# A Flamingo layer on one core: heads kept and scaled in PSUM with two banks, two score banks instead of three, an expert's low part in four pieces, and new order tables

## The reference, cut to what matters

```python
x = x + tanh(g_xattn) * attention(layernorm(x), ctx, ctx, Wq, bq, Wk, bk, Wv, bv, Wo, bo)   # 16 heads of 32
xt = layernorm(x).reshape(4096, 512)
probs = softmax(xt @ router_w + router_b)            # 8 experts
gate, idx = max(probs), argmax(probs)
y = gate * (xt @ expert_w[idx] + expert_b[idx])
x = x + tanh(g_ffn) * y
```

## Time and profile before

| | us |
|---|---|
| median of three executions | 1152.27 |
| the profiled execution | 1165.53 |
| its span, first to last instruction | 1163.8 |

### The profile page before, as it was taken

The page is one execution under the profiler, slowest core; times in us unless marked ns, Lnnn a source line. Parts: engine busy times, 40 slices in busy tenths (PEclk is TensorE's granted clock), DMA queues, the critical chain, the costliest instruction groups (busy, mean ns, idle before and its releaser), DMA issues. The chain is left out here.

```text
span 1163.8 us, 19046 instructions
## 1 busy us (share of the span) xinstructions
PE 1032.3 (89%) x5464; PEld 659.0 (57%) x5464; DVE 805.2 (69%) x1748; ACT 513.1 (44%) x920; POOL 670.6 (58%) x446
## 2 busy tenths in 40 slices
PE   3798899999998999899999998999899765789885
PEld 2554456546754674476457655765565323667674
DVE  5656655876687769767975886588667758686454
ACT  4245624564356345535544454445443435333331
POOL 3046645774587448745874685468545556554453
PEclk9898989999999999999999998999999967999988
DMA  7334222533253334233432432243223712543431
GB/s 231 76 74 121 66 67 68 141 75 98 69 138 78 91 76 134 74 83 91 129 81 73 117 106 74 69 120 104 78 64 90 253 73 81 164 154 120 136 118 46
DMA packets 70884, 119.39 MB, mean 103 GB/s; under 512 B 17854, under 2 KB 18878, under 8 KB 70656
## 3 DMA queue, kind: packets, MB, share of 16 engines
q1 hardware_dynamic: 62496, 98.96, 31.1%
q0 software_dynamic: 6240, 18.68, 5.2%
q10 hardware_dynamic: 2048, 0.53, 0.2%
HBM read 50.42 MB, written 18.66 MB: 59 GB/s over the span
## 5 line engine op out<-in xcount | busy, mean ns | idle before, releaser
L1101 POOL TENSOR_TENSOR psum_keys<-psum_keys,probs 128x1024 f32<-128x1024 f32 x128 | 303.8, 2386 | 120.7 <-ACT probs L691 120.5
L691 ACT ACTIVATE probs<-sc 128x512 f32<-128x512 f32 x512 | 279.4, 598 | 210.5 <-PE sc L499 168.9
L826 DVE TENSOR_REDUCE maxima<-jb 128x1 f32<-128x512 f32 x512 | 323.3, 682 | 69.6 <-PE jb L519 68.6
L1101 POOL TENSOR_TENSOR psum_keys<-probs 128x1024 f32<-128x1024 f32 x64 | 153.5, 2412 | 228.9 <-ACT probs L691 228.9
L519 PE MATMUL jb<-k_stack,q_stack 96*128 96x512 f32 x512 | 197.1, 440 | 26.6 <-DVE maxima L826 10.8
L499 PE MATMUL sc<-q_stack,k_stack 98*128 98x512 f32 x512 | 193.6, 428 | 9.9 <-DMA q_stack<-max_rows 7.9
L519 PEld LDWEIGHTS jb<-k_stack,q_stack 96*128 96x128 f32 x512 | 98.2, 199 | 103.5 <-issue 40.7
L509 PE MATMUL hb<-probs,values 128*32 128x512 f32 x1024 | 141.7, 631 | 16.2 <-DVE heads_raw L845 8.0
L499 PEld LDWEIGHTS sc<-q_stack,k_stack 98*128 98x128 f32 x512 | 95.7, 194 | 82.8 <-ACT probs L691 29.6
L667 PE MATMUL sc<-e_hi,heads_hi 128*128 x156 | 68.6, 440 | 1.4 <-POOL e_lo L1128 0.9
L861 DVE SCALAR_TENSOR_TENSOR k_lo<-jb,bias,k_hi 128x512 fp32r<-128x512 f32 x32 | 23.9, 748 | 64.0 <-ACT k_hi L710 64.0
(11 more groups left out here) (230 smaller groups left out, 1864.0 us busy)
## 6 DMA issues: line engine op xcount, KB each, us to landing
k_stack<-k_hi SPq DMA_DIRECT2D x256, 64.0 KB, 2.0
q_stack<-q_hi SPq DMA_DIRECT2D x256, 64.0 KB, 2.0
stage<-in_x SPq DMA_DIRECT2D x63, 256.0 KB, 3.0
stage<-in_ctx_t SPq DMA_DIRECT2D x32, 256.0 KB, 3.0
k_stack<-k_lo SPq DMA_DIRECT2D x128, 64.0 KB, 2.0
q_stack<-q_lo SPq DMA_DIRECT2D x128, 64.0 KB, 2.0
e_lo<-in_ew SPq DMA_DIRECT2D x8, 1024.0 KB, 12.2
rows<-row SPq DMA_DIRECT2D x30, 257.5 KB
```

What stands on the lines that cost most here:

```text
L691: nc.scalar.activation(probs[:, kt % 2, h, :], scs[(16 * g + n) % NSC][:], ACT.Exp, scale=SCALE)\
L826: nc.vector.tensor_reduce(maxima[g % 2][:, n:n + 1], jbs[j][:], AX.X, ALU.max).then_inc(s["mx_done"], 1)
L1101: nc.gpsimd.tensor_tensor(psum_keys[:, two, :], in0, probs[:, kt % 2, two, :], ALU.add)\
```

## The change

1. There are two banks for heads, `hbs`, and two score banks (NSC = 2). Group g uses bank g % 2, tile n of the experts bank n % 2.
2. NM on VectorE writes its product back into the same PSUM bank; NM on ScalarE and NL on VectorE read it there. `heads_raw` keeps its place only as one of the output tiles.
3. P 0 of group g waits for NL of group g - 2. TO n waits for LO n - 2. HI n waits for OP n of the last batch (for the first four tiles) instead of all four.
4. W on VectorE (an expert's low part) is four instructions of 512 columns; GpSimd's stays one of 2048.
5. All tables are new. The set of steps and the split between VectorE and GpSimd are as before; only the places in the queues differ.

```diff
-NJB, NSC = 4, 3
+NJB, NSC, NHB = 4, 2, 2
@@
-        hb = ps("hb", [P, S])
+        hbs = [ps(f"hb{i}", [P, S]) for i in range(NHB)]
@@ P on TensorE
-                        wait(pe, s["nm_chain"], g)
+                        wait(pe, s["nm_done"], g + 1 - NHB)
...
-                            hb[h * HD:(h + 1) * HD, :], values[:, n, (HG * c + h) * HD:(HG * c + h + 1) * HD],
+                            hbs[g % NHB][h * HD:(h + 1) * HD, :], values[:, n, (HG * c + h) * HD:(HG * c + h + 1) * HD],
@@ TO on TensorE
-                    if n == 0:
-                        wait(pe, s["nm_chain"], NG * B)
+                    if n < NHB:
+                        wait(pe, s["nm_done"], NG * B + n + 1 - NHB)
                     pe.wait_ge(s["xe"], n + 1)
-                    wait(pe, s["lo"], n)
+                    wait(pe, s["lo"], n + 1 - NHB)
@@ NM on ScalarE
-                    nc.scalar.activation(heads_hi[:, c, :], heads_raw[:], ACT.Identity,
+                    nc.scalar.activation(heads_hi[:, c, :], hbs[g % NHB][:], ACT.Identity,
@@ HI on ScalarE
-                    wait(act, s["op_mm"], NT * B)
+                    wait(act, s["op_mm"], NT * (B - 1) + min(n + 1, NT))
@@ NM and NL on VectorE
-                    wait(dve, s["nm_done"], g)
-                    nc.vector.tensor_tensor(heads_raw[:], hb[:], sums[:], ALU.mult).then_inc(s["nm_chain"], 1)
+                    nc.vector.tensor_tensor(hbs[g % NHB][:], hbs[g % NHB][:], sums[:], ALU.mult).then_inc(s["nm_chain"], 1)
...
-                    nc.vector.scalar_tensor_tensor(heads_lo[:, c, :], heads_raw[:], bias[:, 2, c:c + 1],
+                    nc.vector.scalar_tensor_tensor(heads_lo[:, c, :], hbs[g % NHB][:], bias[:, 2, c:c + 1],
@@ W on VectorE
-                    nc.vector.tensor_tensor(e_lo[:, n, :, :], e_lo[:, n, :, :].bitcast(F32), e_hi[:, n, :, :].bitcast(F32),
-                                            ALU.subtract).then_inc(s["ew_lo"], 1)
+                    for k in range(NF):
+                        last = nc.vector.tensor_tensor(e_lo[:, n, k, :], e_lo[:, n, k, :].bitcast(F32),
+                                                       e_hi[:, n, k, :].bitcast(F32), ALU.subtract)
+                    last.then_inc(s["ew_lo"], 1)
```

More of the change, by code:

```diff
@@ L34 @@
     "SP": [
-        "~~RW2 ~~RW3 1SQ ^DC0 1SK 2SQ 2SK ^DC1 ~RW0 ^DC2 ^DC3 ~RW1 ~DR2 ~DR3 3SQ ^DX0 ^DX1 ^DX2 3SK ^DX3 DR0 DR1 ^0SQ",
-        "^0SK",
+        "~~RW3 1SK 2SQ 2SK ^DC0 ^DC1 ~RW0 ~RW1 ^DC2 ^DC3 ~DR2 ~DR3 3SQ ^DX0 ^DX1 3SK ^DX2 ^DX3 DR0 DR1 ^0SQ ^0SK ~RW2",
+        "^1SQ",
     ],
     "PE": [
[10 rows of a table removed]
[10 rows of a table added]
     ],
     "ACT": [
[5 rows of a table removed]
[5 rows of a table added]
     ],
     "DVE": [
[5 rows of a table removed]
[5 rows of a table added]
     ],
     "POOL": [
-        "C3 ~1A3 ~~OP2 ~~OP3 ~1A4 ~1A5 LX0 ~2A0 LX1 ~2A1 LX2 LX3 ~2A2 ~OP0 ~2A3 ~2A4 ~2A5 ~~LR1 ~3A0 ~3A1 ~3A2 ~3A3 ~3A4",
-        "~3A5 ~OP1 0A0 0A1 0A2 0A3 0A4 0A5 ~LR0 1A0 1A1 ^C0 ^C1 ^C2 1A2",
+        "~~2A4 ~~2A5 ~~3A0 ~~3A1 ~~3A2 ~~3A3 ~~3A4 ~~3A5 ~0A0 ~~OP0 ~0A1 ~~OP1 ~0A2 ~0A3 ~0A4 ~0A5 ~~LR0 ~1A0 ~1A1 C0 C1",
+        "C2 ~1A2 C3 ~~OP2 ~1A3 ~~OP3 ~1A4 ~1A5 LX0 LX1 ~2A0 ~2A1 LX2 LX3 ~2A2 ~~LR1 ~2A3",
     ],
@@ L71 @@
     "SP": [
-        "~RW2 ^DC0 ^DC1 LW1 ^DC2 ~RW3 LC ^DC3 ^DX0 LW0 ^DX1 ^DX2 ^DX3 LW2 LW3 ^0SK ^0SQ",
+        "^DC0 ^DC1 LW1 ^DC2 LC ^DC3 ^DX0 ^DX1 ^DX2 LW0 ~RW2 ^DX3 LW2 LW3 ~RW3 ^0SK ^0SQ ^1SQ",
     ],
     "PE": [
[4 rows of a table removed]
[4 rows of a table added]
     ],
     "ACT": [
-        "^C0 ^C1 WT0 TH ^C2 ^C3 WT1 WT2 WT3 ^NX0 WT4 ^0K WT5 WT6 ^NX1 ^T4 ^NX2 ^T5 WT7 ^NX3 ^T6 ^T7 WT8 WT9 WT10 ^0Q WT11",
-        "WT12 WT13 WT14 WT15 ^1Q ^V0 ^0MT ^0MD ^1K ^0E0 ^0E1 ^0E2 ^0E3 ^V1 ^0E4 ^0E5 ^0E6 ^2Q ^0E7 ^V2 ^0E8 ^0E9 ^0E10",
-        "^0E11 ^2K ^0E12 ^0E13 ^0E14",
+        "^C0 ^C1 WT0 ^C2 WT1 WT2 ^C3 WT3 TH ^NX0 ^NX1 ^T4 WT4 ^T5 ^0K ^NX2 ^NX3 WT5 ^T6 ^T7 WT6 WT7 WT8 WT9 WT10 WT11",
+        "WT12 ^0Q WT13 WT14 ^1Q WT15 ^V0 ^0MT ^0MD ^1K ^0E0 ^0E1 ^V1 ^0E2 ^0E3 ^0E4 ^0E5 ^0E6 ^2Q ^0E7 ^V2 ^0E8 ^0E9",
+        "^0E10 ^0E11 ^0E12 ^0E13 ^2K ^0E14",
     ],
     "DVE": [
[3 rows of a table removed]
[3 rows of a table added]
     ],
     "POOL": [
-        "^C0 ^C1 ^C2",
     ],
@@ L96 @@
     "SP": [
-        "~~RW2 ~~RW3 1SQ 1SK ^DC0 ^DC1 2SQ ^DC2 ^DC3 ~DR2 2SK ~RW0 ~DR3 ^DX0 ^DX1 ~RW1 ^DX2 3SQ 3SK ^0SQ ^DX3 ^0SK DR0",
+        "~~RW3 1SK ^DC0 ^DC1 2SQ ^DC2 ^DC3 2SK ~DR2 ~RW0 ~DR3 ~RW1 ^DX0 3SQ ^DX1 ^DX2 ^DX3 ^0SQ DR0 3SK ^0SK",
     ],
     "PE": [
[10 rows of a table removed]
[10 rows of a table added]
     ],
     "ACT": [
[6 rows of a table removed]
[6 rows of a table added]
     ],
     "DVE": [
[5 rows of a table removed]
[5 rows of a table added]
     ],
     "POOL": [
-        "~1A3 C3 ~~OP2 ~~OP3 ~1A4 ~1A5 LX0 ~2A0 LX1 ~2A1 LX2 LX3 ~2A2 ~2A3 ~~LR1 ~OP0 ~2A4 ^LX0 ~2A5 ^C0 ~3A0 ~3A1 ~3A2",
-        "~3A3 ~3A4 ~3A5 0A0 0A1 ~OP1 0A2 0A3 ~LR0 0A4 0A5 ^LX1 1A0 ^C1 ^C2 ~OP2 1A1 1A2 ^C3 ~OP3 1A3 1A4 1A5 2A0 ^LX2 2A1",
-        "^LX3 2A2 2A3",
[4 rows of a table added]
     ],
@@ L134 @@
     "SP": [
-        "W0 ~DR1 ~DR2 W1 W6 W2 W3 W4 W5 ~~RW2 ~DR3 ~~RW3 W7 EB ~RW0 ~RW1 ~RW2 ~RW3",
+        "W0 ~DR1 ~DR2 W1 W6 W2 W3 W4 ~~RW2 ~~RW3 ~DR3 W5 W7 EB ~RW0 ~RW1 ~RW2 ~RW3",
     ],
     "PE": [
[5 rows of a table removed]
[5 rows of a table added]
     ],
     "ACT": [
[4 rows of a table removed]
[4 rows of a table added]
     ],
     "DVE": [
[4 rows of a table removed]
[4 rows of a table added]
     ],
     "POOL": [
[4 rows of a table removed]
[4 rows of a table added]
         "SE37 SE38",
@@ L571, in item @@
                         for k in range(NF):
-                            last = nc.tensor.matmul(hb[h * HD:(h + 1) * HD, 0:E], ones[:], rwc[:, k, :],
+                            last = nc.tensor.matmul(hbs[0][h * HD:(h + 1) * HD, 0:E], ones[:], rwc[:, k, :],
                                                     start=(k == 0), stop=(k == NF - 1))
@@ L647, in item @@
                 elif kind == "TO":
-                    if n == 0:
-                        wait(pe, s["nm_chain"], NG * B)
+                    if n < NHB:
+                        wait(pe, s["nm_done"], NG * B + n + 1 - NHB)
                     pe.wait_ge(s["xe"], n + 1)
-                    wait(pe, s["lo"], n)
+                    wait(pe, s["lo"], n + 1 - NHB)
                     for k in range(NF):
-                        last = nc.tensor.transpose(hb[:, k * P:(k + 1) * P], xe[n % 2][:, k * P:(k + 1) * P], ident[:])
+                        last = nc.tensor.transpose(hbs[n % NHB][:, k * P:(k + 1) * P], xe[n % 2][:, k * P:(k + 1) * P], ident[:])
                     last.then_inc(s["tp"], 1)
@@ L786, in item @@
                     act.wait_ge(s["tp"], n + 1)
-                    wait(act, s["op_mm"], NT * B)
+                    wait(act, s["op_mm"], NT * (B - 1) + min(n + 1, NT))
                     wait(act, s["y"], n + 1 - WORK)
-                    nc.scalar.activation(xt_hi[n % WORK], hb[:, :].rearrange("p (k q) -> p k q", q=P), ACT.Copy)\
+                    nc.scalar.activation(xt_hi[n % WORK], hbs[n % NHB][:, :].rearrange("p (k q) -> p k q", q=P), ACT.Copy)\
                         .then_inc(s["hi"], 1)
@@ L890, in item @@
                     dve.wait_ge(s["cs_mm"], 1)
-                    nc.vector.scalar_tensor_tensor(rwc[:, :, :], hb[:, 0:E].unsqueeze(1).broadcast_to([P, NF, E]), -1.0 / D,
+                    nc.vector.scalar_tensor_tensor(rwc[:, :, :], hbs[0][:, 0:E].unsqueeze(1).broadcast_to([P, NF, E]), -1.0 / D,
                                                    rwc[:, :, :], ALU.mult, ALU.add).then_inc(s["rw_done"], 1)
@@ L1056, in item @@
                     dve.wait_ge(s["hi"], n + 1)
-                    nc.vector.tensor_tensor(xt_lo[n % WORK], hb[:, :].rearrange("p (k q) -> p k q", q=P),
+                    nc.vector.tensor_tensor(xt_lo[n % WORK], hbs[n % NHB][:, :].rearrange("p (k q) -> p k q", q=P),
                                             xt_hi[n % WORK].bitcast(F32), ALU.subtract).then_inc(s["lo"], 1)
```

## The result

The changed kernel takes 1182.08 us (median of three, 1176.0 to 1185.6) where the kernel before takes 1152.27: a ratio of 1.022, with a 95% interval of 1.018 to 1.026. I had forecast 1132 us, with a range up to 1157. Its profiled execution took 1176.0 us, with a span of 1174.2 us. Against the profiled execution before (1165.5 us, span 1163.8) that is 10.5 us more.

What follows compares the result with a forecast made beforehand. The seven middle bodies were taken as bound by TensorE's own queue, the transition and experts' part by waits. The terms +3 -13 +0.4 -10.5 gave -20, so 1152.3 became 1132 us, range 1112 to 1157.

Steps and rivals of the forecast that it cites:

- two banks of scores: Attention bodies: later score-bank release costs 1 us a body, less 0.6 for heads, +3 us over seven; ends -3, +4 a body.
- The rival** on score banks: Bodies: late exponentials make the 2.4 us of stalls count twice, giving 1163 us; decided from 3.3 us a body; chance 0.15.
- the score weights wait over 60 us for exponentials: Sign of being wrong: TensorE's score weights, 29.6 us of waits for exponentials before, would wait over 60 us.
- bodies reach 116 us at full clock: Sign of being wrong, in the attention bodies: 116 us each at full clock, where 111 to 114 us was expected.
- Experts' part: After attention: a second transposing bank removes TensorE's waits for heads_lo and slowed matmuls, -10.5 us; ends 0 and 17 gained.
- 1 for PB: Experts' part: 1 us charged because the third Y waits behind PB with only two score banks.
- The rival on gathers: Experts' part: late gathers make tiles late, so the second bank helps nothing; 1143 us; chance 0.16.
- Transition: End of attention to first expert matmul: no heads_lo stall and earlier planning bring PC 13 us forward, -13 us; ends 5, 18.
- some 20 us of GpSimd's queue follow it in both kernels: Transition: the same GpSimd jobs follow PC in both kernels, so the first expert tile also gains 13 us.
- Pieces: VectorE's e_lo in four operations: +0.2 us for each of six, two on the path, +0.4 us.
- The rival on pieces behind GpSimd: VectorE's e_lo: each piece waits for a GpSimd instruction; three more waits cost 7 us, giving 1139 us; chance 0.12.
- Heads in place: Bodies: multiplying heads in place in PSUM adds nothing on the path; ends -0.1 and +0.1 us each, 3 us in all.

Runs made afterwards that it cites:

- new_order_old_banks: The changed kernel's tables, slightly adapted, with three score banks, one heads bank and heads_raw in the bodies, e_lo in one piece; ratio 1.083 to the kernel before.
- closing_two_and_two: Kernel before; only in the experts' part the third score bank becomes a second transposing bank, leaving two for the experts' matmuls; ratio 1.0075.
- closing_jb: Kernel before; only in the experts' part a small-job bank becomes the second transposing bank, and the experts' matmuls keep three; ratio 0.999.
- nl_later: Kernel before with one heads_lo of the last body moved behind the last group's maxima on VectorE; ratio 0.9968.
- bodies_two_score: Kernel before with scores in two banks instead of three and three steps of P moved ahead of a step of S; 1226 us, ratio 1.054.
- before_exp_quarters: Kernel before with each 512-column exponential of a score bank done as four operations of 128 columns; ratio 1.015.
- after_exp_quarters: Changed kernel, with e_lo in one operation, and each exponential done as four operations of 128 columns; ratio 1.036 to the kernel before.

## Why the prediction was wrong

**The step that failed** is the one on two banks of scores: "I take 1 us a body". A body measured 4 us more. I counted 2.4 us of stalls along TensorE's queue and let the 5 us of idle absorb some. The scores alone cost 2.8 us, so it absorbed none; that those idle moments lie elsewhere (for maxima, projections, DMA) is my reading of the lines. The other 1.6 us, P's waits for late exponentials above all, were not in the count, and by new_order_old_banks they come from the new tables, whose effect on P I had not priced. The upper end, +4 a body, held. **The rival** on score banks named the mechanism, in part, and its threshold of 3.3 us a body was passed. Of the signs of being wrong, "the score weights wait over 60 us for exponentials" came (76.9), and "bodies reach 116 us at full clock" came within 0.1 (115.9). Its 1163 was still too low, because it kept the gain in the experts' part. Its argument that each stall counts twice is not shown; what is shown is 1.6 us of longer occupation, 1.2 and 1.4 of waits and 0.2.

**Experts' part**, -10.5, ends 0 and 17: it came out at +6.3, outside both. The wait that I removed was there and went (16.9 to 2.1 us); I priced the bank that it was taken from at "1 for PB". closing_two_and_two gives that bank's price under the tables of before, 9 us with the gain counted in, and closing_jb shows that even with three banks the gain is nil. The rival on gathers, to which I gave 0.16, was right on the size of that term; its mechanism isn't shown. I had read the two long waits as late gathers myself, and the trace has them behind ScalarE's "remote" waits. (The short ones are eight, not nine.)

**Transition**, -13, ends 5 and 18: 7.7 us. The stall of heads_lo went, its cause as forecast: one SBUF operand fewer. PC came 11.3 us earlier against the bodies (94.1 us behind the last one, 105.4 before), near the 13. What failed is "some 20 us of GpSimd's queue follow it in both kernels": 20.3 us before, 23.9 in the changed kernel, where the first expert matmul waits for an e_lo of VectorE that stands behind one of 6.34 us. Taking the stall away alone gives 3.7 us (nl_later), not 5.84. In the changed kernel TensorE still idles 4.45 us for the maxima's DMA and 5.62 for PA:

```profile
947.16 1.22 PE L499 MATMUL sc<-q_stack,k_stack 98*128 98x512 f32 x2 [4.45 <-DMA q_stack<-max_rows]
...
975.46 1.04 PE L635 MATMUL jb<-early_room 128*128 128x21 f32 x4 [5.62 <-DVE early_room L1006]
```

**Pieces**, +0.4: 3.9 us under the tables of before, not shown under the new ones. The rival on pieces behind GpSimd had the sign and the place, and was worth about half of its 7. GPSIMD Engine Reference in the Trainium skill, section Key points, says that GpSimd contends with VectorE's instructions that have two SBUF inputs; the trace agrees, with 6.22 us beside GpSimd's sums and 2.48 alone for the same four pieces, while heads_lo with one PSUM input stays below 0.76. That the contention is the cause is the page's word; the runs show the times.

**Heads in place**, nothing: right. heads_lo measured 742 ns in the median, as q_lo's row said. VectorE: DVE Perf Modes in the Trainium skill, section on the TRN2 errata, would add 65 ns by an estimate; no such step shows between 743 and 742.

The sum of the two profiled executions: the opening, to the last exponential of the first group, is 2.9 us shorter (78.4 against 81.3; I had 0), seven bodies take 805.2 us against 790.5, +14.7, transition -7.7, experts' part +6.3: 10.4 us. The 790.5 are not typical. Two bodies were 7.5 us long, and the first took 112.1 us at a clock of 0.91, where nl_later has 107.3 and closing_jb 107.0 at 0.95 with the same tables; that is 12.5 of the 13.2 us by which this execution stands above its median. So the bodies cost some 27 us, by an estimate from these rows, and of the forecast's miss of 50 us 24 are in them, 17 in the experts' part and 5 in the transition. The changed kernel's 6.1 us between profile and median were not traced to a place.

## What to carry to other kernels

A buffer that is given to one stage is taken from another: price the loss by running the old kernel with the smaller set, before counting what the larger one gains. Here that price (66 us) was an upper one: with an order made for the smaller set the scores cost some 20 us in seven bodies. A stall counted along the bound engine's queue need not be covered by that engine's idle time elsewhere. And a wait that ends at a full buffer may only hide the next one (here ScalarE's late start), so a removed wait is worth what the second-latest event leaves. Read such a wait back to its first cause, not only to the next engine.

## What the runs showed that I had not expected

- Splitting an operation of two SBUF inputs into four cost over 2 us beside GpSimd: 6.22 and 6.63 us instead of 3.88 and 4.43 whole, but 2.48 against 2.28 alone.
- Short waits of TensorE cost more than themselves: in bodies_two_score the 602 matmuls of a body took 111.9 us busy instead of 106.7, with the granted clock at 0.97 in the mean. Not all of it is the clock: the changed kernel's body has 108.3 at 1.00.
- The experts' part was only 154.7 us long in before_exp_quarters (166.3 before), with the same closing tables, and 158.9 in after_exp_quarters. In the kernel before ScalarE waits three times there for an event that the profile puts to another core or an unknown queue, and four times, 22.7 us, in closing_jb; with quarters there is none in either kernel. What it is was not settled, and it may be what bounds this part. The waits view of the kernel before, in that part:

```profile
ACT heads_hi L789 <- remote: 10.4, 2, 5.2
ACT gbo L783 <- remote: 4.4, 1, 4.4
```
